# A four-layer conditional kernel: index lists, weight transfers and attention masks put in other places

## The reference, cut to what matters

```
x = x + L0(x, W0[id_b])              # one 32x32 matrix per batch, over the token axis
x = x + L1(x)                        # paged attention, 8 heads, 4 kv groups, head 32, window 128
x = x + L2(x)                        # x@Wbase + ((x@Wt)@A[e_b])@B[e_b]@Wp * scaling[e_b]
x = x + L3(x, W3[subject_b])         # one 32x32 matrix per batch, over the token axis
# L1: q, k, v from x; rms norm and rotary embedding of q and k;
k_blocks = k_blocks.at[blk, :, off, :].set(k)     # new keys and values go into a paged cache
v_blocks = v_blocks.at[blk, :, off, :].set(v)
allowed  = (kpos <= pos) & (kpos > pos - 128)
scores   = where(allowed, q.k_all * 256**-0.5, -inf);  o = softmax(scores) @ v_all;  x += o @ Wo
```

## Time and profile before

| | before |
|---|---|
| median of 3 runs | 226.25 us |
| the profiled execution | 226.22 us |
| its span | 224.3 us |
| VectorE busy | 177.9 us, 79% |
| TensorE matmul busy | 194.2 us, 87% |
| ScalarE busy | 132.7 us, 59% |
| bytes moved | 28.98 MB, mean 129 GB/s |

### The profile page before, as it was taken

One profiled execution on the slowest core, in us unless ns is written; L12 is line 12 of the kernel. 1 busy time (PEld: TensorE's weight loads), 2 busy tenths in 40 slices (PEclk: granted clock), 3 DMA queues, 4 the chain that ended last, 5 costly groups with the idle time before them and its releaser, 6 DMA issues.

```text
span 224.3 us, 6913 instructions
## 1 busy us (share of the span) xinstructions
PE 194.2 (87%) x2383; PEld 150.6 (67%) x2383; DVE 177.9 (79%) x466; ACT 132.7 (59%) x496; POOL 81.6 (36%) x103
## 2 busy tenths in 40 slices
PE   0479929997999939996999999799999999999982
PEld 0455615775656628785788788688888888888660
DVE  5888961289599998549899999799999899999740
ACT  5115422304359991678767966777779767885610
POOL 5403004000277776721443464166335634420010
PEclk9999985969999997999999999999999999999999
DMA  3479999940022445541314543454446435521011
GB/s 95 141 180 257 218 203 402 253 139 7 19 81 77 159 159 143 139 153 35 107 48 129 154 132 88 143 163 109 140 144 178 113 121 156 159 69 29 29 53 47
DMA packets 20803, 28.98 MB, mean 129 GB/s; under 512 B 10669, under 2 KB 16056, under 8 KB 20386
## 3 DMA queue, kind: packets, MB, share of 16 engines
q0 software_dynamic: 6992, 18.00, 27.9%
q1 hardware_dynamic: 12738, 9.60, 15.4%
q10 hardware_dynamic: 1040, 0.95, 1.5%
HBM read 28.31 MB, written 7.64 MB: 160 GB/s over the span
## 4 chain that ended last, share of the span: by engine, by line
PE 68%; DMA 11%; SPq 6%; ACT 6%; issue 3%; DVE 3%; POOL 0%; ACTq 0%; DVEq 0%; POOLq 0%
PE bank L1266 13%; PE quad L1280 11%; PE quad L1233 9%; DMA xin<-in_x 6%; PE quad L1204 6%; PE bank L1312 5%; PE bank L1328 4%; PE bank L1262 3%; PE quad L1302 3%; PE bank L1197 3%; PE bank L1295 3%; PE bank L1220 3%; PE bank L1321 2%; DMA out<-x4s 2%; DMA yall<-in_w,scratch 2%
## 5 line engine op out<-in xcount | busy, mean ns | idle before, releaser
L768 ACT ACTIVATE work<-bank,nmx 128x164 f32<-128x164 f32 x128 | 49.9, 408 | 26.8 <-DVE nmx L1055 26.8
L1266 PE MATMUL bank<-kt_rope,big 128*128 128x164 f32 x256 | 43.4, 303 | 0.0
L1266 PEld LDWEIGHTS bank<-kt_rope,big 128*128 128x128 f32 x256 | 39.7, 190 | 3.9
L603 POOL DMA_INDIRECT big<-merged,idx x16 | 16.4, 1022 | 45.9 <-DMA big<-in_pool,idx 26.8
L1065 DVE STREAM_TRANSPOSE work<-work 128x768 f32<-128x768 f32 (+1 forms) x64 | 32.7, 547 | 0.0
L1233 PE MATMUL quad<-wqkv_sb,yall 128*128 128x512 f32 x64 | 32.4, 631 | 0.0
L1055 DVE TENSOR_REDUCE nmx<-bank 128x3 f32<-128x492 f32 (+1 forms) x48 | 28.4, 591 | 3.8 <-PE bank L1266 3.3
L768 ACT ACTIVATION_READ_ACCUMULATOR work<-bank,nmx 128x1 f32 x128 | 27.5, 215 | 0.0
L747 ACT ACTIVATE big<-qT,con 128x256 f32<-128x256 f32 x64 | 27.1, 500 | 0.0
L576 POOL DMA_INDIRECT merged<-qT,idx x16 | 16.6, 1039 | 27.3 <-DVEq L967 22.2
L1072 DVE TENSOR_TENSOR onT<-quad,rT 32x256 f32<-32x256 f32 (+1 forms) x48 | 19.9, 414 | 8.0 <-PE quad L1280 7.0
(11 more groups left out here) (158 smaller groups left out, 342.1 us busy)
## 6 DMA issues: line engine op xcount, KB each, us to landing
xin<-in_x SPq DMA_DIRECT2D x16, 128.0 KB, 8.3
merged<-big SPq DMA_DIRECT2D x2, 1024.0 KB, 10.8
out<-x4s SPq DMA_DIRECT2D x16, 128.0 KB, 2.2
merged<-own SPq DMA_DIRECT2D x1, 1024.0 KB, 12.9
w3bd<-w_scratch SPq DMA_DIRECT2D x64, 4.0 KB, 2.4
wqkv_sb<-in_wqkv ACTq DMA_DIRECT2D x1, 512.0 KB, 4.2
w_scratch<-yall SPq DMA_DIRECT2D x1, 256.0 KB, 3.1
wt_sb<-in_wt SPq DMA_DIRECT2D x1, 256.0 KB, 2.8
```

The costliest lines, as they stand in the source:

```text
L768: act.activation(prob[:, p, hd, 0:NK], ps_sc[(p + i) % 2][:, j * NK:j * NK + NK], ACT.Exp, bias=nmx[:, p, hd:hd + 1], scale=1.0, accum_out ...
L1266: mm = pe.matmul(at[:, j * NK:j * NK + NK], qbd[:, p, hd, :], kT[:, p, hd // GSZ, 0:NK], start=False, stop=(j == n - 1), skip_group_check= ...
```

## The change

- The adapter weights `wt`, `at`, `bt`, `wp` are issued by ScalarE at the very start, and TensorE computes `inward` before tile 0; it does not wait for the L0 matrices before its first matmuls. 4 warming matmuls stand where 9 did.
- `wbase` and `wo` are issued ahead of x tiles 4 and 5. GpSimd issues two of the transfers of `w0i` that ScalarE issued.
- The 2 MB gather into `stage` waits until x tile 7 has landed; x tiles 8 to 11 and the small tables are issued ahead of it or beside it.
- `outward` moves from TensorE step 9 to 5, `canonical` from 8 to 6. `by_batch` goes: a transfer on SP's queue takes the row of 704 numbers to 64 partitions, and SP waits for ScalarE's copy (`s_canoned`) before it issues that and the writes of `merged` behind it.
- `lists_of_rows` has 7 instructions where it had 11. It and `shifted_lists` stand behind VectorE's step 4, `rows_of_tiles` behind step 5.
- The masks leave ScalarE. VectorE makes them with comparisons, four tiles at a time in two instructions: the first four tiles between the phases, the others in attention steps 0, 1 and 2. `LATER` is 5 where it was 6.
- One item moves from within phase 1 to `AFTERWARDS`.

```diff
-        LATER = 6
+        LATER = 5
-        INLINE.update({9: ITEMS[0:4], 12: ITEMS[4:5], 14: ITEMS[5:6], 16: ITEMS[6:7]})
-        AFTERWARDS = ITEMS[7:-3]
+        INLINE.update({9: ITEMS[0:3], 12: ITEMS[3:4], 14: ITEMS[4:5], 16: ITEMS[5:6]})
+        AFTERWARDS = ITEMS[6:-3]
@@ SP: behind the first two blocks_of(...)
+            for dst, src in ((wbase_sb[:, :, :], wbase.rearrange("(c p) n -> p c n", p=128)),
+                             (wo_rows[:, :, :], wo.rearrange("(c p) n -> p c n", p=128))):
+                sp.dma_start(dst, src).then_inc(s_wout, 16)
+            fetch_x(4, 6)
             for b in range(NB):
                 dst, src = blocks_of(b, AGAIN, NT)
                 sp.dma_start(dst, src).then_inc(s_w0[SOON + 1], 16)
-            fetch_x(4, 6)
...
+            fetch_x(6, XRING + 4)
+            sp.dma_start(con[:, COL["later"][1]:NCONST], ...).then_inc(s_conm, 16)
...
-            fetch_x(XRING, XRING + 4)
+            sp.wait_ge(s_canoned, 2)
+            sp.dma_start(canon, canon_row.rearrange("p (b i) -> p b i", i=SPAN)).then_inc(s_canonical, 16)
+            sp.wait_ge(s_big, 1)
+            sp.dma_start(merged[B * BLOCK:2 * B * BLOCK, :]..., own...).then_inc(s_init, 16)
             for i in range(2):
                 sp.wait_ge(s_stage[i], 16)
                 sp.dma_start(merged_blocks[2 * B * i:2 * B * i + B, :], stage[:, i, :]).then_inc(s_init, 16)
@@ GpSimd
+            wait(s_w0d, 16)
+            for b in range(2, NB):
+                dst, src = blocks_of(b, SOON, AGAIN)
+                pl.dma_start(dst, src).then_inc(s_w0p[1], 16)
+            wait(s_wout, 32)
+            ... (the two additions of ident to wbase_sb, before the gather now)
             wait(s_tab, 16)
-            wait(s_blkr, 16)
-            for i in range(SOON + 2):
-                wait(s_w0[i], 16 * PIECES[i])
+            wait(s_x[XRING - 1], 16)
@@ ScalarE
+            (wt, at, bt, wp)  act.dma_start(dst, src).then_inc(s_wpre, 16)     # behind the first transfer
-                if s == 8:
+                if s == 1:
+                    all_blocks()
+                if s == 5:
+                    outward()
+                if s == 6:
                     act.wait_ge(s_ipe, 2)      # copies canonical's row
-                if s == 6:
+                if s == 3:
                     inward()
-                if s == 9:
-                    outward()
-                if 12 <= s < 12 + PAIRS: ... masks(t)
@@ VectorE
+                ve.wait_ge(s_canonical, 16)
+                link(ve.tensor_scalar(cmiss, canon, 0.0, MISS, ALU.is_equal, ALU.mult))
+                link(ve.scalar_tensor_tensor(out=canon, in0=canon, scalar=-1.0, in1=cmiss, op0=ALU.add, op1=ALU.add))
+                for rows, name, per, n in ((rows4[:, 1, :], "m4", 4, 9), (rows2, "m8", 8, OWN), (rows1, "m16", 16, OWN)):
+                    ... one scalar_tensor_tensor each
-            AFTER = {0: (same_blocks,), 2: (segments,), 5: (lists_of_rows, shifted_lists), 7: (rows_of_tiles,)}
+            AFTER = {0: (same_blocks,), 2: (segments,), 4: (lists_of_rows, shifted_lists), 5: (rows_of_tiles,)}
+            def masks(part_of_tiles):
+                t0, t1 = RING * part_of_tiles, RING * part_of_tiles + RING
+                for k, (name, a, b, op) in enumerate((("backpos", 0, NKB, ALU.is_lt), ("ownpos", NKB, NK, ALU.is_gt))):
+                    ve.tensor_tensor(mask[:, t0:t1, a:b], cc(name).unsqueeze(1).broadcast_to([128, RING, b - a]),
+                                     pos3[:, k, t0:t1].unsqueeze(2).broadcast_to([128, RING, b - a]), op
+                                     ).then_inc(mask_done, 1)
+            masks(0)                              # between the phases
+                if 0 <= t < RING - 1:             # attention steps 0, 1, 2
+                    masks(t + 1)
@@ TensorE
-            INDEX = {5: (dead_tokens,), 6: (inward,), 8: (canonical,), 9: (by_batch, outward), 10: (tiles,)}
+            INDEX = {5: (outward, dead_tokens), 6: (canonical,), 10: (tiles,)}
-            pe.wait_ge(s_awpad, 1)
-            pe.wait_ge(w0g_done, 1)
-            for i in range(9):
+            inward()
+            pe.wait_ge(s_blank, 3)
+            for i in range(4):
```

More of the change, by code:

```diff
@@ L39 @@
 BIG = float(2 ** 20)
+MISS = float(2 ** 12)
 NEG = -1e30
@@ L452, in _ @@
             sp.dma_start(w3e[:, :, :], w3.rearrange("n c d -> c n d")).then_inc(s_w3e, 16)
-            fetch_x(XRING, XRING + 4)
+            sp.wait_ge(s_canoned, 2)
+            sp.dma_start(canon, canon_row.rearrange("p (b i) -> p b i", i=SPAN)).then_inc(s_canonical, 16)
+            sp.wait_ge(s_big, 1)
+            sp.dma_start(merged[B * BLOCK:2 * B * BLOCK, :].rearrange("(p f) n -> p f n", p=128),
+                         own[:, :, :].rearrange("p r (f n) -> p (r f) n", n=ROW)).then_inc(s_init, 16)
             for i in range(2):
@@ L456, in _ @@
                 sp.dma_start(merged_blocks[2 * B * i:2 * B * i + B, :], stage[:, i, :]).then_inc(s_init, 16)
-            sp.wait_ge(s_big, 1)
-            sp.dma_start(merged[B * BLOCK:2 * B * BLOCK, :].rearrange("(p f) n -> p f n", p=128),
-                         own[:, :, :].rearrange("p r (f n) -> p (r f) n", n=ROW)).then_inc(s_init, 16)
             fetch_x(XRING + 4, NT)
@@ L533, in _ @@
                 dst, src = block_of(b, 1)
-                pl.dma_start(dst, src).then_inc(s_w0p, 16)
+                pl.dma_start(dst, src).then_inc(s_w0p[0], 16)
+            wait(s_w0d, 16)
[3 more added lines that the diff above has]
+            wait(s_wout, 32)
+            wait(s_con, 16)
+            for c in range(2):
+                pl.tensor_tensor(wbase_sb[:, c, 128 * c:128 * c + 128],
+                                 wbase_sb[:, c, 128 * c:128 * c + 128], ident, ALU.add).then_inc(s_wb, 1)
             wait(s_tab, 16)
-            wait(s_blkr, 16)
-            for i in range(SOON + 2):
-                wait(s_w0[i], 16 * PIECES[i])
+            wait(s_x[XRING - 1], 16)
             for i, j in enumerate((0, 2)):
@@ L544, in _ @@
                     bounds_check=NPOOL - 1, oob_is_err=False, engine_sem=desc_init).then_inc(s_stage[i], 16)
-            wait(s_wout, 32)
-            wait(s_con, 16)
-            for c in range(2):
-                pl.tensor_tensor(wbase_sb[:, c, 128 * c:128 * c + 128],
-                                 wbase_sb[:, c, 128 * c:128 * c + 128], ident, ALU.add).then_inc(s_wb, 1)
             wait(s_num, 32)
@@ L690, in copied @@
                     act.copy(yall[:, 2 * p:2 * p + 2, :], ps_y.rearrange("p (t n) -> p t n", t=2)).then_inc(y_copied, 1)
-            def masks(t):
-                for k, (name, a, b, sign) in enumerate((("backpos", 0, NKB, -1.0), ("ownpos", NKB, NK, 1.0))):
-                    act.activation(mask[:, t, a:b], cc(name), ACT.Relu, bias=pos3[:, k, t:t + 1], scale=sign
-                                   ).then_inc(mask_done, 1)
             def phase1(h, u):
@@ L729, in phase1 @@
                                    ).then_inc(rt_done, 1)
-                if 12 <= s < 12 + PAIRS:
-                    if s == 12:
-                        act.wait_ge(s_rows, 1)
-                        act.wait_ge(s_conm, 16)
-                    for t in (2 * (s - 12), 2 * (s - 12) + 1):
-                        masks(t)
-            for s in range(12 + PAIRS):
+            for s in range(NT + 3):
                 phase1(s // RING, s % RING)
@@ L1170, in canonical @@
                                        start=(j == 0), stop=(j == OWN - 1))
-                mm.then_inc(s_ipe, 1)
-            def by_batch():
-                pe.wait_ge(s_canoned, 2)
-                for i in range(SPAN):
-                    mm = pe.matmul(ps_idx[0:B, 400 + i:401 + i], canon_row.rearrange("p (b i) -> p i b", i=SPAN)[:, i],
-                                   ident[0:1, 0:1], start=True, stop=True)
                 mm.then_inc(s_ipe, 1)
@@ L1237, in phase1 @@
                         inputs(kind, pair)
[L1239 to L1242 removed]
+            inward()
+            pe.wait_ge(s_blank, 3)
+            for i in range(4):
+                pe.matmul(ps_y[:, 0:128], aow[:, 0, :], aow[:, 1, :], start=True, stop=True)
             for s in range(NT + 2):
```

67 lines of the change are left out of this document (25 added, 42 removed).

## The result

The changed kernel takes 219.17 us, the median of 4 runs (217.43 to 220.16); the kernel before took 226.39 beside it (225.89 to 228.49). The ratio is 0.9655, 95% interval 0.9566 to 0.9745: 7.2 us less. The profiled execution took 218.61 us, its span is 216.8. The forecast was 215.6. The experiments ran on three chips, and there the kernel before spread from 221 to 239 us. I compare medians of one chip and, above all, places in the traces.

What follows compares the result with a forecast made beforehand. VectorE carries phase 1: the end of the lists sets the end of phase 1, which sets the attention's start. Lists -10.3, between the phases -1.4, attention steps +1.1: -10.6 us on 226.22 gives 215.6 us, range 212.5 to 220.5.

Steps and rivals of the forecast that it cites:

- the case that had 0.52: Canonical row lands when the 2 MB gather is over, taken as 35.5 us; time 214.5 to 217.5 us, chance 0.52.
- rival 2: Something late costs the gain: row landing, `s_init`, or masks at double price; 217.5 to 221.6 us, chance 0.22.
- the upper bound of 41.5: Worst landing of the canonical row, if it takes 12.0 us like the 32 KB of w3e beside the gather.
- the signs of being wrong: First tile over 1.5 us later, gather's end moved over 3 us, or TensorE's items unfinished when first keys are ready.
- The start: Four weight transfers (640 KB) beside the gather of the L0 matrices: 0.5 us taken, between 0 and 2.3.
- The bound above: Most the early weights could delay the start: 640 KB at 148 GB/s, 4.3 us, some 2 before the L0 gather: 2.3.
- The gather's start: 2 MB gather issued once x tile 7 has landed: 21.8 us, where 18.79 stood.
- The lists: Making the lists on VectorE: 11 instructions become 7, so 7.6 us becomes 6.8; they end at 42.3, against 52.6.
- from L to E: From the end of the lists to the end of phase 1: 29.3 us again, so phase 1 ends at 71.6.
- The scatters: GpSimd's first scatter near 47, with `s_rows` at 45.8 and `s_init` about 46; 2.5 us of slack at the last.
- The masks: Masks moved to VectorE, 1.0 us a pair: 1.4 us gained between the phases, 1.1 lost in the attention steps.
- The sum: -10.3 for earlier lists, -1.4 between the phases, +1.1 in attention: -10.6 us on 226.22, giving 215.6.

Runs made afterwards that it cites:

- weights later: Changed kernel with ScalarE issuing the four adapter weights near 12 us and `inward` in TensorE's step 4: 225.00 us, 3.0 above the changed kernel there.
- weights on SP: Changed kernel with adapter weights on SP behind tile 2's matrices, `inward` in step 4, tile 2's matrices by ScalarE: 219.64 us (1 of 4; others 224.65 to 226.28).
- x tiles first as well: Changed kernel with adapter weights on SP behind tile 2's matrices, and x tiles 6 and 7 ahead of the later tiles' matrices: 223.89 us.

## Why the prediction was nearly right, point by point

*The direction and the mechanism.* Right. x tile 6 no longer waits behind the gather, `by_batch` is gone, and the row lands with the end of the gather: the case that had 0.52. The wait of VectorE for it is 2.07 us (2.1 forecast), the landing 6.16 us after the issue (6.0). The time is another matter: 219.17 lies outside the 214.5 to 217.5 us that I gave this case, in the band of rival 2 (217.5 to 221.6), by a row that landed at 39.70 between my 35.5 and the upper bound of 41.5. Two of the signs of being wrong that I had named came true: the first tile starts 3.0 us later (the sign was 1.5), and the gather's end, 39.4, is 4.6 us behind my 34.8 (the sign was 3). I had weighed a rule of the Trainium skill there (DMA: Bandwidth & Descriptors, Queues, rings and completion order): each DMA engine takes turns between its queues packet by packet. From it I drew that the small transfer would pass the gather. The traces don't bear that out here: the row took 3.9 to 7.7 us behind the whole gather, and 1.8, 2.1 and 3.2 us where the gather or its second half was held back. Why it waits is not shown; I only know what it waits for.

*The start* is the step that failed: "The 16 engines are far from busy there, so I take 0.5 us". The bound above was 2.3. Measured, GpSimd's addition to the L0 matrices ends at 11.78, and at 8.55 before: 3.2 us, beyond the bound. The edits show it as the weights' price from both sides: put later, the weights give tile 0 back at 17.94 and 16.98, and put early in the kernel before they move it to 20.89. And the engines weren't far from busy: windows of the kernel before and of the changed one (columns as in the earlier trace rows) have a DMA share of 0.74 and 0.88 from 4 to 9 us.

```profile
4.00:9.00 5.00, 0.31 (x1) 0.34 (x2) 3.49 (x11) 0.00 (x0) 2.74 (x5) 1.00 0.74 229
```
```profile
4.00:9.00 5.00, 0.00 (x0) 0.00 (x0) 1.58 (x7) 1.71 (x1) 2.17 (x4) 1.00 0.88 266
```

*The gather's start.* I had 21.8, it was 25.63, 3.8 later. SP issues the matrices before the x tiles, so the start's delay reaches tile 7: issued at 22.25, where I had 19.2. It landed 2.5 us later, as forecast, and the other 0.8 us is a term that I left out: from that landing, 24.75, to the start of GpSimd's gather instruction it took 0.9 us. From there the gather took what I had forecast: 14.1 us from 25.63 to the row's landing, against 13.7. So the missing 4.2 us (39.70 against 35.5) are 3.8 of a late gather and 0.4 of its length, and the start is the larger part of the 3.8 in this kernel. It is no simple sum, though: where the start was mended, the gather came at 24.41 (weights later), 24.71 (weights on SP) and 23.78 (x tiles first as well), never at 21.8. In the last two tile 7 took 3.2 and 4.5 us to land, where the changed kernel has 2.5. That fits an account by which the 640 KB have to pass somewhere before tile 7, and my sum had them pass for almost nothing. It is not shown: the 512 KB of `wbase` and `wo`, which the change also puts there, stood ahead of tile 7 in every one of these kernels.

*Tile 2's matrices on GpSimd's queue.* I had priced nothing. TensorE waited 1.38 us for them and VectorE 1.85 before tile 3. The wait for the row covers it: with them on ScalarE, VectorE waits 0.86 us before tile 3 and 3.28 us for the row, and the lists are no sooner.

*The lists* took 6.8 us, as forecast; *from L to E* 29.2 (29.3). In all twelve traces with early lists, E is 26.2 to 26.8 us behind the lists in idx, once the idle time that ScalarE's stretches gave VectorE is taken off.

*The scatters.* The first was released by VectorE's `s_rows` at 50.75, 4 us later than forecast as all else. `s_init` was late by as much (49.6, where I had 46), so earlier lists alone would have met it next. With x tiles 6 and 7 first the first scatter, at 50.10, did wait for a write of `merged`, and with half of the gather held it came 6 us later still. *The masks.* A pair takes 0.87 us (1.0 forecast), 0.65 and 0.30 for the two. E to the first maxima went from 14.98 to 13.95 us, 1.0 gained where I took 1.4; the third maxima came 1.8 sooner (1.6). The attention steps 1 and 2 took 0.15 and 0.80 us more than before, not 0.5 and 1.0. With the shorter step 5 it comes to 0.5 lost over the first seven steps (1.1 forecast). Behind E it is 1.3 us gained, against 0.3.

*The sum.* Forecast 215.6; 4.2 later at the lists, 1.2 less behind: 218.6, the profiled execution. That the total came within 3.6 us of the median owes something to luck: the two misses have opposite signs.

What stays open: whether the lists 1.8 us sooner (x tiles 6 and 7 first) reach the end. By E, 26.3 us behind the lists, they should, and the first scatter was at 50.10; but that kernel was timed only on a chip where ScalarE's idle stretches hid such a difference. Why the row of "weights on SP" landed 1.4 us behind the gather. And what the idle stretches are.

## What to carry to other kernels

A transfer is early only if its bytes find the DMA engines free: 640 KB issued at the start cost the first indirect gather 3.2 us, and one queue's order carried the delay on to the next gather. Before pricing an earlier start, ask which landing the next stage waits for: where it is the end of a large gather, work before it that gets faster only lengthens the wait, and holding the gather back moves the wait to whoever reads the gathered rows.

## What the runs showed of the hardware

- A 2.8 KB transfer on SP's queue, issued 5.6 to 8.5 us behind the second half of a 2 MB indirect gather on GpSimd's queue, landed 12.4 to 13.4 us after that half was issued, in all nine traces that have this order; in eight of them that is 0.1 to 0.4 us behind the landing of the half. With no gather ahead of it, it took 1.8 us.
- 640 KB of transfers issued beside a 256 KB indirect gather stretched it from 4.5 to 7.8 us (8.0 us where they were the kernel before's only alteration); with those transfers issued later it took 4.0 to 4.7 us in four variants of the changed kernel.
- ScalarE stood idle for 1.9 to 6.2 us between 58 and 78 us, with "remote" in place of an engine or a transfer that ends it, in all eight traces of the first and second chip, and in none of the third chip, nor in the first traces of the two kernels. The changed kernel's median was 2.8 to 3.6 us higher where it occurs (221.98 against 219.17 and 218.34); how much of that is due to it is not shown.
- With the halves of the gather apart, the first 1 MB took 8.4 and 8.5 us with x tiles beside it, and the second, as large, took 12.5 and 11.3 us beside the writes of `merged`.
